# The end of the first experts and the projections of the second layer, from seven blocks to one

## The reference, cut to what matters

```
x = _layernorm(x + _L0_ffn_ref(...))   # inside: layernorm(residual + fused) * ln_gamma + ln_beta
qkv = x @ qkv_w + qkv_b                # 128 -> 3 * 128
q, k, v = jnp.split(qkv, 3, axis=-1)   # q, k as 16 heads of 8
q = q / (norm(q over a head) + 1e-06) * qn_scale + qn_bias
k = k / (norm(k over a head) + 1e-06) * kn_scale + kn_bias
h = swish(k @ gate) * (k @ val); pred = h @ proj; loss = mean((pred - v) ** 2)   # two training steps
o = (swish(q @ gate) * (q @ val)) @ proj @ proj_w + proj_b
```

## Time and profile before

| | us |
|---|---|
| median of three runs | 2275.29 (2271.91 to 2281.7) |
| the profiled execution's own time | 2276.86 |
| its span in the profile | 2275.1 |
| DVE busy, of the span | 1646.6 (72%) |
| PE busy | 1834.8 (81%) |
| ACT busy | 1215.9 (53%) |
| POOL busy | 578.4 (25%) |

### The profile page before, as it was taken

How to read it: one execution, slowest core, us unless ns; L and a number is a source line. 1 busy time by engine, 2 the same in 40 slices (tenths; PEclk the granted TensorE clock), 3 DMA queues, 4 the chain that set the end, 5 groups by cost and what they waited for, 6 DMA issues and landing times. The chain is left out here.

```text
span 2275.1 us, 35126 instructions
## 1 busy us (share of the span) xinstructions
PE 1834.8 (81%) x11438; PEld 1493.1 (66%) x11438; DVE 1646.6 (72%) x4042; ACT 1215.9 (53%) x2830; POOL 578.4 (25%) x620
## 2 busy tenths in 40 slices
PE   6999999999999999964671328999799988743771
PEld 4888888888888888753571326777677766622760
DVE  5999999999999999856556676776577755557433
ACT  5888888888888888834452313332233323231332
POOL 0111111111111111103456163442144401000472
PEclk9999999999999999966886659999999999965995
DMA  7000000000000000032542000000000000040343
GB/s 216 1 1 1 1 1 1 1 1 1 1 1 2 1 1 1 1 86 46 101 113 55 26 0 1 0 0 1 1 1 0 0 1 3 2 133 9 91 90 86
DMA packets 64471, 61.42 MB, mean 27 GB/s; under 512 B 10672, under 2 KB 54160, under 8 KB 64192
## 3 DMA queue, kind: packets, MB, share of 16 engines
q1 hardware_dynamic: 53936, 42.80, 6.4%
q0 software_dynamic: 10384, 16.72, 4.5%
HBM read 40.38 MB, written 18.86 MB: 26 GB/s over the span
## 5 line engine op out<-in xcount | busy, mean ns | idle before, releaser
L521 DVE TENSOR_TENSOR probT<-turn_ps,probT 128x512 fp32r<-128x512 f32 x512 | 335.2, 686 | 63.2 <-ACT probT L435 63.1
L450 ACT ACTIVATE prob<-prob,negmax 128x512 f32<-128x512 f32 x512 | 375.3, 739 | 5.8 <-DVE negmax L515 5.8
L269 POOL TENSOR_TENSOR x<-x,scaled 128x512 f32<-128x512 f32 x128 | 167.0, 1305 | 812.7 <-DVE scaled L536 812.7
L515 DVE CUSTOM_DVE_ANT_0 prob<-score_ps,bias 128x512 f32<-128x512 f32 x512 | 341.0, 684 | 6.8 <-issue 1.1
L435 ACT CAST probT<-turn_ps 128x512 fp32r<-128x512 f32 x512 | 283.7, 598 | 21.9 <-PE turn_ps L341 21.9
L341 PE MATMUL turn_ps<-ident,prob 128*128 128x128 f32 x2048 | 266.3, 273 | 1.3 <-DVE probT L521 1.1
L358 PE MATMUL work_ps<-probT,val 128*128 128x512 f32 x1024 | 257.1, 393 | 0.1
L341 PEld LDWEIGHTS turn_ps<-ident,prob 128*128 128x128 f32 x2048 | 236.8, 140 | 28.2 <-DVE probT L521 3.5
L329 PE MATMUL score_ps<-k,q 64*128 64x512 f32 x1536 | 215.3, 412 | 3.5 <-DVE negmax L515 2.1
L358 PEld LDWEIGHTS work_ps<-probT,val 128*128 128x128 f32 x1024 | 187.4, 188 | 39.9 <-DVE probT L521 1.8
L329 PEld LDWEIGHTS score_ps<-k,q 64*128 64x128 f32 x1536 | 136.9, 186 | 48.6 <-issue 19.7
(11 more groups left out here) (497 smaller groups left out, 4044.6 us busy)
## 6 DMA issues: line engine op xcount, KB each, us to landing
ew<-L_ffn_fc_weight SPq DMA_DIRECT2D x32, 256.0 KB
bias<-bias_line SPq DMA_DIRECT2D x16, 448.0 KB, 11.5
mid_rows<-row SPq DMA_DIRECT2D x40, 128.5 KB
last_rows<-row SPq DMA_DIRECT2D x40, 64.0 KB
rows_dram<-rows SPq DMA_DIRECT2D x1, 2304.0 KB, 18.7
acc_dram<-zero POOLq DMA_DIRECT2D x1, 2112.0 KB, 16.8
acc<-acc_dram SPq DMA_DIRECT2D x4, 528.0 KB, 6.1
x_rows<-x SPq DMA_DIRECT2D x4, 512.0 KB, 6.6
```

Source lines behind the costliest of these rows:

```text
L269: pool.tensor_tensor(mine, mine, scaled[a][:, :, :], ALU.add).then_inc(added, 1)
L450: act.activation(mine, mine, ACT.Exp, bias=negmax[p % 2][:, i, a:a + 1], scale=-1.0, accum_out=total[p % 4][:, i, a:a + 1]).then_inc(exp_d ...
L515: dve.tensor_tensor_reduce(prob[p % 2][a][:, i, :], score_ps[i % 2][a][:, :], bias[:, h, first:first + SEQ][:, ::-1], -1.0, 3.0e38, ALU.ad ...
L521: dve.tensor_tensor(probT[1][:, g % QT, :], turn_ps[g % 2][:, :], probT[0][:, g % QT, :].bitcast(F32), ALU.subtract).then_inc(turned_lo, 1)
```

## The change

Blocks 1 and 3 to 6 become one, `finish_and_project`, and the tensors of the ttt layer are allocated before the experts (`home_ttt`). The loop has steps s = 0 to 4. In step s group s (8 tiles) is normalized twice with `Norms`, while group s - 1 is projected in four pairs of tiles. Each engine's list names both kinds of work in a fixed order.

The head norm's scale is folded into a second copy of the weights and biases of queries and keys (512 columns: 256 plain ones for the length, 256 scaled ones for the result); the bias is added by PE with a product of two rows in fp32r (high and low part). ACT squares out of PSUM; DVE writes inverse times scaled product to qk. The shift of the keys is a bias column in ACT's and DVE's split of the turned keys; qk itself gets it afterwards for the keys. The queries get theirs in `transpose_parts`. The weights are fetched, proj is turned and the bias split in the same block, ahead of the loop. `end_of_phase` now stands behind it.

Around the change: `apart_sq` in `places_0` becomes BF16.

```
 def transpose_parts(core, src, shift, parts, ident):
...
-                act.copy(hi[:, c * 512:(c + 1) * 512], flat(bank[c % 4][:, :, :])).then_inc(hi_ready, 1)
+                act.activation(hi[:, c * 512:(c + 1) * 512], flat(bank[c % 4][:, :, :]), ACT.Identity, bias=shift).then_inc(hi_ready, 1)
...
-                dve.tensor_tensor(lo[...], flat(bank[c % 4][:, :, :]), hi[...].bitcast(F32), ALU.subtract).then_inc(lo_ready, 1)
+                dve.scalar_tensor_tensor(lo[...], flat(bank[c % 4][:, :, :]), shift, hi[...].bitcast(F32), ALU.add, ALU.subtract).then_inc(lo_ready, 1)
...
+def finish_and_project(core, ins, keep, gamma, beta):
...
+            # gpsimd
+            inner.constants(pool)
+            outer.constants(pool)
+            fetch(0)
+            pool.memset(tiny[:, :], 1e-6).then_inc(ones_ready, 1)
+            pool.memset(ones[:, :], 1.0).then_inc(ones_ready, 1)
+            pool.iota(halves[:, :], ...).then_inc(ones_ready, 1)
+            pool.wait_ge(small_in, 64)
+            for i, wide in enumerate((scale, shift, scale, shift)):
+                pool.tensor_copy(half, small[:, i, :]...).then_inc(laid, 1)
+            for g in range(1, GROUPS):
+                fetch(g)
...
+            # tensor
+            def project(p):
+                for t in (2 * p, 2 * p + 1):
+                    if t >= 4:
+                        pe.wait_ge(unit, t - 3)
+                    pe.matmul(qk_ps[t % 4][:, :], xT[c % 2][:, mine], w[:, 0:V_AT], start=True, stop=False)
+                    pe.matmul(qk_ps[t % 4][:, :], ones_r[:, :], b_parts[:, 0:V_AT], start=False, stop=True).then_inc(qk_done, 1)
+                    pe.matmul(v_ps[c % 2][:, mine], xT[c % 2][:, mine], w[:, V_AT:], start=True, stop=False)
+                    mm = pe.matmul(v_ps[c % 2][:, mine], ones_r[:, :], b_parts[:, V_AT:], start=False, stop=True)
+            for g in range(GROUPS):
+                turn_x(2 * g); project(4 * g)
+                if g >= 1: turn_k(2 * g - 1)
+                turn_x(2 * g + 1); project(4 * g + 1); project(4 * g + 2)
+                turn_k(2 * g); project(4 * g + 3)
+            turn_k(CHUNKS - 1)
...
+            # scalar, step s: g = s - 1, p = 4 * g; the parts of group s only for s < 4, those of g only for s >= 1
+            inner.root(s); root(p - 1); squares(p); copy_v(2 * g - 1); copy_k(2 * g - 1); copy_x(2 * g + 1)
+            inside(s, 0); root(p); squares(p + 1); inside(s, 1); root(p + 1); copy_v(2 * g); squares(p + 2)
+            outer.root(s); copy_k(2 * g); outside(s, 0); root(p + 2); squares(p + 3); copy_x(2 * s); outside(s, 1)
...
+            # vector, ahead of the loop
+            for g in range(GROUPS):
+                dve.tensor_tensor(x[:, of(g), :], x[:, of(g), :], along(beta[:, :], G), ALU.add).then_inc(plus_ready, 1)
+            dve.wait_ge(laid, 4)
+            ... (w scaled, b scaled, b_parts, projT copied)
+            # vector, step s
+            see_inner(2 * s); see_inner(2 * s + 1); spread(inner, s); divide(p - 1); settle(inner, s); measure(p)
+            rest_of_k(2 * g - 1); divide(p); shape(2 * s); measure(p + 1); see_outer(2 * s); shape(2 * s + 1)
+            divide(p + 1); see_outer(2 * s + 1); spread(outer, s); measure(p + 2); settle(outer, s)
+            rest_of_k(2 * g); divide(p + 2); measure(p + 3)
...
+            def divide(p):
+                dve.wait_ge(raised, p + 1)
+                dve.reciprocal(inv[:, 2 * p:2 * p + 2, :], length[:, 2 * p:2 * p + 2, :]).then_inc(inv_ready, 1)
+                dve.wait_ge(inv_ready, p + 1)
+                for t in (2 * p, 2 * p + 1):
+                    dve.tensor_tensor(by_head(qk[:, t, :]), by_head(qk_ps[t % 4][:, 2 * D:4 * D]), inv[:, t, :]..., ALU.mult).then_inc(unit, 1)
```

More of the change, by code:

```diff
@@ L131, with transpose_parts @@
 BIAS_W = SEQ + (SEQ // P - 1) * P
[L134 to L166, removed]
+def transpose_parts(core, src, shift, parts, ident):
     nc = core.nc
@@ L1007, in _, with home_ttt @@
                 sp.wait_ge(sent[r], 16 * (SLOT_TILES // ROW_RING))
-def finish_0(core, keep, gamma, beta):
+TTT_HEADS, HD = 16, 8
+HID = 512
+HC = HID // P
+def home_ttt(core, st, keep):
+    keep["gate"], keep["val"], keep["projT"] = (core.sb(st, n, [P, HID]) for n in ("gate", "valw", "projT"))
+    keep["proj"] = core.sb(st, "proj", [P, HC, D])
+    keep["qk"], keep["v"] = core.sb(st, "qk", [P, TILES, 2 * D]), core.sb(st, "v", [P, TILES, D])
+    keep["ones"], keep["shift_columns"] = core.sb(st, "ones", [P, P]), core.sb(st, "shift_columns", [P, 2])
+    keep["k_parts"] = keep["q_parts"] = [core.sb(st, f"turned_{half}", [P, N_TOK], F32R) for half in ("hi", "lo")]
@@ new lines, in spread, with settle, shape @@
+            def spread(norms, g):
+                for k in range(5):
+                    norms.moments(dve, g, k)
+            def settle(norms, g):
+                norms.moments(dve, g, 6)
+                norms.moments(dve, g, 7)
+            def shape(c):
+                mine = f[:, 4 * c:4 * c + 4, :]
+                dve.wait_ge(by_inner, 4 * (c + 1))
+                dve.tensor_tensor(mine, mine, along(gamma[:, :], 4), ALU.mult).then_inc(shaped, 1)
+                dve.wait_ge(shaped, c + 1)
+                dve.wait_ge(plus_ready, c // 2 + 1)
+                dve.tensor_tensor(mine, mine, x[:, 4 * c:4 * c + 4, :], ALU.add).then_inc(summed, 1)
@@ new lines, in _ @@
+            dve.tensor_copy(keep["projT"][:, :], k_ps[:, :]).then_inc(proj_copied, 1)
+            dve.wait_ge(columns_ready, 2)
+            for s in range(GROUPS + 1):
+                g, p = s - 1, 4 * (s - 1)
+                normal, projected = s < GROUPS, s >= 1
+                if normal:
+                    see_inner(2 * s)
+                    see_inner(2 * s + 1)
+                    spread(inner, s)
+                if g >= 1:
+                    divide(p - 1)
+                if normal:
+                    settle(inner, s)
+                if projected:
+                    measure(p)
+                if g >= 1:
+                    rest_of_k(2 * g - 1)
+                if projected:
+                    divide(p)
+                if normal:
+                    shape(2 * s)
+                if projected:
+                    measure(p + 1)
+                if normal:
+                    see_outer(2 * s)
+                    shape(2 * s + 1)
+                if projected:
+                    divide(p + 1)
+                if normal:
+                    see_outer(2 * s + 1)
+                    spread(outer, s)
+                if projected:
+                    measure(p + 2)
+                if normal:
+                    settle(outer, s)
+                if projected:
+                    rest_of_k(2 * g)
+                    divide(p + 2)
+                    measure(p + 3)
@@ L1108, in enter_ffn_0 @@
+            divide(4 * GROUPS - 1)
+            rest_of_k(CHUNKS - 1)
 def enter_ffn_0(core, ins, keep, gamma, beta):
```

436 lines of the change are left out of this document (215 added, 221 removed).

## The result

| | before | after |
|---|---|---|
| median | 2275.68 us (20 runs, 2265.49 to 2281.70) | 2260.65 us (20 runs, 2247.93 to 2272.05) |
| profiled execution, own time | 2276.86 | 2256.59 |
| from the first sum to the gradient phase | 161.4 | 141.6 |

The ratio is 0.9937 (95% interval 0.9923 to 0.9951): faster, clear of the noise, by about 15 us, half of the forecast 30. It lies in the range, 2233 to 2262, near its slow end. The profiled execution is one of the faster of the 20: it took 20.3 us less than the profiled one before, 19.8 of them in the replaced stretch, where the medians differ by 15.

A forecast was written before the change was run, and what follows sets the result against it. A chain of blocks, each bound by DVE plus its waits, was taken as the bound. 1225 + 105 + 8 + 1.5 = 1339.5 against 1369.8, minus 0.2, saves 30 us: median 2245, range 2233 to 2262.

The forecast's parts named there:

- PE's term: Projection on PE: 1.4 us a tile, 12.8 us a group at full clock and 25.6 at half.
- the walk: Following the ordered engine lists through the new loop: steps of 23.3 us, 105 in all; 27 a step at half clock.
- The clock term: PE's clock in the new loop: half clock throughout would add 18 us, of which 8 were taken.
- The rule that I weighed: Small PE idle times between matmul groups make the clock swing; by it all 18 us are paid, saving 20.
- Rival (a): PE's clock stays at half in the new loop: saving 20 us, 2255 us; chance 0.18.
- Rival (d): Two-row bias products at four-pass price and half clock: 4.8 us a tile, 34 us slower, 2309; chance 0.04.
- the first bn_stats: Start of the replaced stretch: normalizing on DVE begins at 1225 us (1224 to 1227).
- the first step: First loop step, norms only: 11.3 us until DVE can start the second group.
- DVE's busy time: DVE busy some 82 us between the first gather and the first gradient product.
- the end of the phase: Clearing and barrier behind the new block: 1.5 us, the same as before, so no saving.
- rival (b): No clock loss and shorter handings over in the loop: steps of 22 us, saving 43, 2232 us; chance 0.12.
- The small edits: apart_sq in bf16: 0 us, bounds -1 and +1; bias column in the queries' split: +0.2 us, at most +1.

The follow-up runs named there:

- again: The changed kernel itself, unchanged, profiled and timed a second time: ratio to the kernel before 0.9899.
- rows64: The changed kernel with bias products over 64 rows (62 of them zero) instead of two: ratio to the kernel before 0.9895, 2256.3 us.
- rows96: The changed kernel with bias products over 96 rows (94 of them zero) instead of two: ratio to the kernel before 0.9842, 2244.6 us.
- rows128: The changed kernel with bias products over 128 rows (126 of them zero) instead of two: ratio to the kernel before 0.9800, 2204.5 us.
- again_b: The changed kernel once more, unchanged, on a later chip: ratio to the kernel before 0.9927, median 2258.9 us.
- paced: The changed kernel, two-row bias products kept, with gathers of the third and fourth group held until ACT has written xT: ratio to before 0.9938, 2263.4 us.
- warm12: The changed kernel with 12 unused f32 products of 128x512 ahead of the loop in PE's list: ratio to the kernel before 0.9939.
- regroup: The changed kernel with both wide products of a tile first, then both bias products: ratio to the kernel before 0.9847.
- no_bias: The changed kernel with the two bias products of each tile left out: ratio to the kernel before 0.9791.
- one_row_f32_paced: The changed kernel with held gathers and bias products of one row in plain f32 instead of two in fp32r: ratio to before 1.0276, 2339.4 us.
- rows128_b: The changed kernel with 128-row bias products, run again on another chip: ratio to the kernel before 0.9861, 2246.8 us.
- rows128_paced: The changed kernel with 128-row bias products and gathers of the third and fourth group held until ACT has written xT: ratio to before 0.9813, 2234.8 us.
- first group's chip: The chip of the first four follow-up runs, on which the kernel before took 2251 us.

## Why the prediction was wrong

**The step that failed** is PE's term: "a tile's 512 + 128 columns take 1.10 us, its two bias rows in fp32r 0.23 and about 0.06: 1.4 ... I take the fp32r row, as the instruction is the same". It measured 2.15 us at full clock and 3.8 at half, with 2.8 foretold. The doubt was named (fp32r price at best, "at worst as four-pass f32, 1.1 a tile" for the bias; it came to 1.05 in all, 0.75 more than taken), and its cause was another than the four-pass price: no column took longer, but the loads of weights of 64 rows or less, between products of 128, start late. With all eight tiles at half clock a group is 8 x 3.85 + 3.4 = 34 us of PE, and that is the 35-us step of again, where the walk had 27 for half clock. So PE, not DVE, was the longest engine, for as long as the clock was low. More than 64 rows give the kernel 12 us back (rows64 to rows96) to 26 (again to rows128). The missing 15 us lie between the two, so the cause is shown; why the load starts late is not.

**The clock term** failed with it. 8 us were taken of 18 (as printed, 27 for 23.3 in two steps and 4 and 5 more add up to 16.4), from PE's idle stretches. PE had few idle stretches, and the clock stayed at 0.50 for 52 us. That is no constant of the kernel. In the seven profiles with products of two or 64 rows the clock first rises 9 to 10 us behind the first projection (again_b, paced, warm12, rows64) or only after 49, 69 and 80 (after, regroup, again), and between the first and the last projection it is low for 25 to 81 us. In the eight with 96 or 128 rows and in no_bias it rises after 3 to 6 us and is low for 15 to 33; with one row of f32 it never rises. So the rows of the bias products have a part in it, as far as one profile of each can show, and something else decides between 10 and 80 us, which the runs leave open. PE's busy time alone does not: the two rows shown above have 0.50 and 0.99 with 11.3 of 12 us busy.

The rule that I weighed, the Trainium skill's "A second HAM failure mode: psum-queue depth-cycling", names small idle times between groups of matmuls as the danger. Swings of that kind are in the traces: in rows128, where PE idles between its groups, the clock falls three times after its first rise, for some 10 us in all. In the kernel after, it does not fall once between its rise and the last projection. What was large there, the late rise, that rule does not name, so its sum (a saving of 20) is nearer to the 15 than mine by another mechanism.

**Rival (a)**, half clock to the end at 2255, came nearest in number, partly by luck: the clock was low for half of the stretch only, and a higher tile price stood in place of the rest. **Rival (d)** had the right place, the bias products of two rows, with a wrong mechanism and size. Something of its kind is one_row_f32_paced, whose tile of 5.3 us is above its 3.7 and 4.8: +62 us.

**ACT's wait** was in no step. Taking it away gives 12 us where the tile price is low (rows128_b to rows128_paced), and nothing measurable where the two-row products stand (again_b to paced).

**What held**: the first bn_stats (1225 foretold, 1224.6), the first step (11.3, 11.1), DVE's busy time (82, 79), the end of the phase, nothing outside the stretch, and the walk itself: with 128 rows and no wait of ACT the first bn_stats and the last rest_of_k are 99 to 100 us apart (rows128, rows128_paced and its repeat), where 105 + 8 had been worked out. The steps there are 22 us instead of 23.3, as in rival (b). That rows128_b saves 30 us, just the forecast, is two errors that cancel: ACT's wait of 12 us was not foretold, and walk and clock term were too dear by as much.

**The small edits**: the squares that ACT writes in bf16 take 387 ns each, as before in f32. A bias column adds 94 ns to ACT's split (589 before, 683 after), 0.1 foretold.

**The best version** is 128 rows with held gathers: 2230.6 us and a ratio of 0.9792, 28 us below the changed kernel in the same group, at the cost of 126 rows of zeros and a wait ahead of two of the four groups of gathers.

## What to carry to other kernels

A product over few rows is priced by its neighbours: before folding a bias or a constant into TensorE as a product of one or two rows between full ones, fill it up with zeros (96 and 128 rows were enough here, 64 were not), or at least put such products next to each other, which halved the price. Look at the distance from one tile's start to the next, not at the durations. Where a kernel's executions scatter, compare the granted clock of several of them before explaining one profile: the same stretch of the same kernel had 0.50 in one and 0.99 in another. And in a stage that issues gathers far ahead of need, look for waits without a releaser on an engine that has nothing to do with them, and hold the gathers back once.

## What was not expected of the hardware

- Weights of 2 or 64 rows between products of 128 rows: a tile takes 2.15 to 2.16 us (full clock) instead of 1.37 with 128 rows and 1.38 to 1.45 with 96. Four changes a tile cost 0.78 us, two 0.40. The wide bias product's load starts late.
- The granted clock depends on more than PE's busy share: 0.50 with PE busy 177 of 180 us (one row), 1.00 with 5.28 of 8 us (rows128, one window), and 0.50 or 0.99 with 11.3 of 12 us in two executions of one kernel.
- With 96 or 128 rows the clock rises 3 to 6 us behind the first projection, with 2 or 64 rows after 9 to 80, and the times scatter over 12 to 24 us instead of 3 to 7. Why stays open.
- ACT idle for 5 to 10 us with its input ready, during a run of 24 gathers or just behind it, on two chips and in the profile of the result, and in no run of the first group's chip; gone on both when the gathers are held. What it waits for stays open.
- The chips differ in stages with many gathers: 202 against 234 us for the expert stage of the same kernel.
